# Two expert stages re-ordered around eight head groups of gated linear attention, with the keys' low halves ahead of the decayed scores

## The reference, cut to what matters

```python
x = x + 0.5 * ffn(layernorm(x)); x = x + attn(layernorm(x)); x = x + 0.5 * ffn(layernorm(x))

def ffn(h):                                     # 64 experts, 8 kept
    scores = softmax(h @ router_weight.T + router_bias)
    w, idx = top_k(scores, 8)
    return h * w.sum() + scatter(w, idx) @ expert_bias

def attn(h):                                    # 32 heads in 8 groups (one key and value head each), 16 chunks of 128
    q, k = rope(h @ Wq.T), rope(h @ Wk.T);  v = h @ Wv.T
    dt = softplus(h @ Win.T + dt_bias);  g = -dt * exp(A_log_bias);  G = cumsum(g in the chunk)
    xc = v * dt
    y = (q k.T * exp(G_i - G_j) masked) @ xc + (q * exp(G)) @ state
    state = state * exp(G_last) + (k * exp(G_last - G)).T @ xc
    return (rms_norm(y) * gnorm_w * silu(h @ Wg.T)) @ Wo.T
```

## Time and profile before

| | |
|---|---|
| median of 3 runs | 1793.26 us (1790.17 to 1793.82) |
| profiled execution | 1792.12 us, span 1790.3 us |
| TensorE busy | 1680.6 us (94%), mean granted clock 0.975 |
| VectorE, ScalarE, GpSimd busy | 1442.7, 1138.8, 1209.0 us |
| the chain that ended last | TensorE 68%, GpSimd 15%, issue 7%, VectorE 5%, ScalarE 5% |

### The profile page before, as it was taken

The page is one execution under the profiler, slowest core; times in us unless marked ns, Lnnn a source line. Parts: engine busy times, 40 slices in busy tenths (PEclk is TensorE's granted clock), DMA queues, the critical chain, the costliest instruction groups (busy, mean ns, idle before and its releaser), DMA issues.

```text
span 1790.3 us, 34879 instructions
## 1 busy us (share of the span) xinstructions
PE 1680.6 (94%) x11652; PEld 964.7 (54%) x11652; DVE 1442.7 (81%) x3157; ACT 1138.8 (64%) x3012; POOL 1209.0 (68%) x1139
## 2 busy tenths in 40 slices
PE   5667999999999999999999999999999999999976
PEld 4443555555555555555555555555555555555544
DVE  6984888888887878888897878787887888788876
ACT  5445666666666667666676666666766667666643
POOL 1225767776777768777777777776777768777633
PEclk9778999999999999999999999999999999999997
DMA  4110101110110101110121102110111111110002
GB/s 176 36 35 20 48 19 60 45 45 21 34 56 34 48 25 54 48 48 19 34 68 36 37 19 70 38 42 25 43 60 30 36 33 57 37 36 21 23 1 94
DMA packets 38481, 76.69 MB, mean 43 GB/s; under 512 B 4768, under 2 KB 5792, under 8 KB 37152
## 3 DMA queue, kind: packets, MB, share of 16 engines
q1 hardware_dynamic: 38304, 74.47, 13.2%
HBM read 69.99 MB, written 4.46 MB: 42 GB/s over the span
## 4 chain that ended last, share of the span: by engine, by line
PE 68%; POOL 15%; issue 7%; DVE 5%; ACT 5%; DMA 0%; SPq 0%; POOLq 0%; ACTq 0%; DVEq 0%
PE B L298 21%; PE B L300 21%; PE B L299 21%; PE B L784 3%; POOL WL L1099 3%; POOL QS L1105 2%; POOL PL L1140 2%; POOL ROWS L1118 1%; POOL WVF L1128 1%; POOL RR L1147 1%; POOL QL L1110 1%; ACT XN L417 1%; ACT QS L893 1%; ACT PF L931 1%; POOL WVL L1136 1%
## 5 line engine op out<-in xcount | busy, mean ns | idle before, releaser
L1140 POOL TENSOR_TENSOR PL<-PF,PH 128x512 bf16<-128x512 f32 x128 | 158.1, 1235 | 314.3 <-ACT PH L937 314.3
L298 PE MATMUL B<-WH,XTH 128*128 128x512 bf16 (+1 forms) x1024 | 282.6, 300 | 2.2 <-POOL WL L1099 2.2
L299 PE MATMUL B<-WL,XTH 128*128 128x512 bf16 (+1 forms) x1024 | 282.5, 300 | 0.0
L300 PE MATMUL B<-WH,XTL 128*128 128x512 bf16 (+1 forms) x1024 | 282.5, 300 | 0.0
L937 ACT ACTIVATE PH<-PF 128x512 bf16<-128x512 f32 x128 | 80.8, 631 | 276.0 <-DVE PF L1309 276.0
L298 PE MATMUL B<-XTH,WH 128*128 128x512 bf16 x640 | 243.3, 380 | 4.2 <-DVE QF L1275 3.5
L1105 POOL TENSOR_TENSOR QS<-QS,SIN 128x512 f32<-128x512 f32 x160 | 204.4, 1278 | 61.6 <-ACT QS L893 61.6
L299 PE MATMUL B<-XTL,WH 128*128 128x512 bf16 x640 | 243.3, 380 | 0.0
L300 PE MATMUL B<-XTH,WL 128*128 128x512 bf16 x640 | 243.1, 380 | 0.0
L1359 DVE SCALAR_TENSOR_TENSOR YF<-B,RR,G 128x128 f32<-128x128 f32 x512 | 144.0, 344 | 73.1 <-POOL RR L1147 73.1
L1309 DVE SCALAR_TENSOR_TENSOR PF<-B,DT,PF 128x128 f32<-128x128 f32 x512 | 143.4, 341 | 68.9 <-PE B L300 56.4
(11 more groups left out here) (158 smaller groups left out, 4464.8 us busy)
## 6 DMA issues: line engine op xcount, KB each, us to landing
ROWS<-rows_dram SPq DMA_DIRECT2D x128, 256.0 KB, 3.3
STAGE<-in_wall SPq DMA_DIRECT2D x112, 256.0 KB, 2.8
ACC<-in_x SPq DMA_DIRECT2D x4, 1024.0 KB, 9.4
out<-ACC SPq DMA_DIRECT2D x3, 1024.0 KB, 3.9
COS<-in_cos SPq DMA_DIRECT2D x1, 1024.0 KB, 13.7
SIN<-in_sin SPq DMA_DIRECT2D x1, 1024.0 KB, 16.4
out<-ACC SPq DMA_DIRECT2D x4, 256.0 KB, 2.0
EBF<-in_eb SPq DMA_DIRECT2D x1, 256.0 KB, 4.3
```

Of the source, the lines that this page charges most:

```text
L298: nc.tensor.matmul(out_, ah, bh, start=first, stop=False)
L299: nc.tensor.matmul(out_, ah, bl, start=False, stop=False)
L300: return nc.tensor.matmul(out_, al, bh, start=False, stop=last)
L1140: nc.gpsimd.tensor_tensor(PL[:, n % 2, :], PF[:, :], PH[:, n % 2, :], ALU.subtract).then_inc(pl_ready.sem, 1)
```

## The change

Steady steps: VectorE's `keys_lo` goes ahead of `decayed`. The three ring banks are renamed, the order of output banks in the last block changes. In the last group statistics of blocks NB and NB + 1 move into chunks 6 to 11, normalising, turns, copies and logits of block NB into chunks 12 to 15, and in these `wv_hi` goes behind `state_hi`. XN and XNT get buffers of their own (TXN, TXNT) in the memory of XTH and XTL.

```diff
@@ VectorE, ScalarE, TensorE: step
+                if s == 3 and now:
+                    keys_lo(g, b + 1)
                 if nxt:
                     decayed(g, n + 1)
...
-                if s == 3 and now:
-                    keys_lo(g, b + 1)
...
-                if last and n >= NCH - BLK:
-                    dve_stats(dve, 0, NB, (n - NCH + BLK,))
+                if last and BLK + 2 <= n < 2 * BLK + 2:
+                    dve_stats(dve, 0, NB, (n - BLK - 2,))
+                if last and 2 * BLK + 2 <= n < 3 * BLK:
+                    dve_stats(dve, 0, NB + 1, (2 * (n - 2 * BLK - 2), 2 * (n - 2 * BLK - 2) + 1))
...
+                if last and n == NCH - 4:
+                    act_normalise(act, 0, NB, (0, 1, 2))
+                if last and n == NCH - 3:
+                    act_turned(act, NB, (0,))
+                    act_normalise(act, 0, NB, (3,))
+                if last and n in (NCH - 3, NCH - 2):
+                    act_turned(act, NB, (n - NCH + 4,))
                 if nxt:
                     p_hi(g, n + 1)
...
-                if nxt:
+                ending = last and n >= NCH - BLK
+                if nxt and not ending:
                     wv_hi(g, n + 1)
...
                 square(g, n)
                 state_hi(g, n)
+                if nxt and ending:
+                    wv_hi(g, n + 1)
...
+                if last and n == NCH - 3:
+                    pe.wait_ge(out_free.sem, out_free.at(g, 2 * BLK + 1))
+                    pe_turn(pe, NB, (0,))
                 read_state(g, n)
+                if last and n in (NCH - 3, NCH - 2):
+                    pe_turn(pe, NB, (n - NCH + 4,))
+                if last and n == NCH - 1:
+                    pe_logits(pe, NB, (0,))
```

```diff
+            for i in range(BLK):
+                sp.dma_start(ACC[:, i, :], x[0][:, i, :]).then_inc(x0_landed[i].sem, 16)
+            sp.dma_start(IDF[:, :], masks[:, 2 * P:3 * P]).then_inc(id_landed.sem, 16)
...
+            nc.gpsimd.memset(WH[:, NPIECE - 1, :], 0.0).then_inc(zero_ready.sem, 1)
...
+            pe.wait_ge(zero_ready.sem, 1)
+            for i in range(28):
+                nc.tensor.matmul(B_T[:, :], WH[:, NPIECE - 1, 0:P], WH[:, NPIECE - 1, :], start=True, stop=True)
+            pe.wait_ge(id_landed.sem, 16)
+            pe_turn(pe, 0)
+            pe.wait_ge(router_landed.sem, 32)
+            pe_logits(pe, 0)
+            pe_turn(pe, 1)
+            pe.wait_ge(const_dve.sem, 6)
+            pe.wait_ge(const_act.sem, 2)
+            for k in range(NB):
+                if k:
+                    pe_turn2(pe, k - 1)
+                pe_weights(pe, k)
+                if 1 <= k < NB - 1:
+                    pe_turn(pe, k + 1)
+                pe_mix(pe, k)
+                if k + 1 < NB:
+                    pe_logits(pe, k + 1)
+                if k:
+                    pe_dt(pe, k - 1)
+                if k == NB - 1:
+                    pe.wait_ge(f_l.sem, f_l.at(NB - 1, 0))
+                    for item in range(2):
+                        fill(0, 0, item, None, True, 0)
...
+            pe_turn2(pe, NB - 1)
+            pe_dt(pe, NB - 1)
+            pe_sums(pe, 0)
+            for item in range(2, NFILL):
                 fill(0, 0, item, None, True, 0)
+                if item % 2 == 0:
+                    pe_rows(pe, item // 2 - 1)
+                elif item < NFILL - 1:
+                    pe_sums(pe, item // 2)
@@ ScalarE
             for k in range(NB):
                 act_exp(act, k)
+                if k:
+                    act_normalise(act, 1, k - 1)
+                    act_turned2(act, k - 1)
+                if k == 0:
+                    act_turned(act, 1)
+                act_weights(act, k)
+                if 1 <= k < NB - 1:
                     act_turned(act, k + 1)
+                for i in (2 * k, 2 * k + 1):
+                    split_hi(0, i)
                 if k + 2 < NB:
                     act_normalise(act, 0, k + 2)
@@ GpSimd
             for k in range(NB):
+                for i in range(BLK):
+                    pool_sum(pool, k, i)
+                pool_rstd(pool, 1, k)
+                pool.wait_ge(f_s8.sem, f_s8.at(min(k + 1, NB - 1), 0))
+                for i in (2 * k, 2 * k + 1):
                     split_lo(0, i)
@@ VectorE
+            dve_stats(dve, 0, 2)
+            dve_gate(dve, 0)
             dve.wait_ge(const_act.sem, 2)
...
+            dve_stats(dve, 0, 3)
+            dve_mixed(dve, 0)
+            dve_stats(dve, 1, 0)
+            for k in range(1, NB):
                 dve_gate(dve, k)
+                dve_turned2(dve, k - 1)
+                dve_mixed(dve, k)
+                if k == NB - 1:
+                    dve_dt_in(dve, 0)
                 dve_stats(dve, 1, k)
+            dve_dt(dve, 0)
+            dve_turned2(dve, NB - 1)
```

```diff
@@ TensorE
             for f in range(NB, 2 * NB):
                 if f + 1 < 2 * NB:
+                    if f == NB:
+                        pe.wait_ge(st_ready.sem, st_ready.at(KVH - 1, cs_event(NCH - 2)))
+                        pe.wait_ge(inter_read.sem, inter_read.at(KVH - 1, in_event(NCH - 1)))
                     pe_turn(pe, f + 1)
+                    pe_logits(pe, f + 1)
...
                 pe_weights(pe, f)
                 pe_mix(pe, f)
-                if f + 1 < 2 * NB:
-                    pe_logits(pe, f + 1)
+                if f == NB:
+                    project_out(KVH - 1, NCH - 1, True)
@@ ScalarE
+            act_normalise(act, 0, NB + 1)
             zt_hi(KVH - 1, NCH - 1)
             for f in range(NB, 2 * NB):
+                if f == NB:
+                    act_turned(act, f + 1)
                 act_exp(act, f)
+                if NB < f < 2 * NB - 1:
                     act_turned(act, f + 1)
                 act_weights(act, f)
+                if f + 2 < 2 * NB:
+                    act_normalise(act, 0, f + 2)
@@ VectorE
+            dve_stats(dve, 0, NB + 2, (0, 1))
+            dve_gate(dve, NB)
             zt_lo(KVH - 1, NCH - 1)
             add_out(KVH - 1, NCH - 2, True)
+            dve_stats(dve, 0, NB + 2, (2, 3))
+            dve_mixed(dve, NB)
+            dve_gate(dve, NB + 1)
             add_out(KVH - 1, NCH - 1, True)
+            dve_stats(dve, 0, NB + 3)
+            dve_mixed(dve, NB + 1)
+            dve_gate(dve, NB + 2)
+            dve_gate(dve, NB + 3)
+            dve_mixed(dve, NB + 2)
+            dve_mixed(dve, NB + 3, (0, 1))
+            dve_last(dve, NB + 3, (2, 3))
```

More of the change, by code:

```diff
@@ L132, in build @@
         ACC = sb("ACC", [P, NCH, HID])
+        with ExitStack() as over:
+            TXN = over.enter_context(nc.sbuf_tensor("TXN", [P, 3, BLK, HID], F32))
+            TXNT = over.enter_context(nc.sbuf_tensor("TXNT", [P, BLK, HID], F32))
         XTH = sb("XTH", [P, KT, L], BF16)
@@ L414, in act_normalise @@
                 act.wait_ge(f_acc.sem, f_acc.at(f - 2, 3))
             A = chunks_of(f)
[L416 to L422 removed]
+            for i in chunks:
+                into = xnt(f, i) if w else xn(f, i)
+                nc.scalar.activation(into, A[:, i, :], ACT.Identity, bias=NMR[:, w, f % 2, i:i + 1],
+                                     scale=RSTD[:, w, f % 2, i:i + 1]).then_inc(f_xn[w].sem, 1)
@@ L423, in pe_turn @@
+        def pe_turn(pe, f, chunks=range(BLK)):
+            for i in chunks:
                 pe.wait_ge(f_xn[0].sem, f_xn[0].at(f, i))
@@ L426, in pe_turn @@
                     pe.wait_ge(f_xtl.sem, f_xtl.at(f - 2, i))
+                elif f == 1:
+                    pe.wait_ge(f_xnt.sem, f_xnt.at(0, i))
+                elif f == NB and i:
+                    pe.wait_ge(f_xnt.sem, f_xnt.at(NB, i - 1))
                 elif f >= NB + 2:
                     pe.wait_ge(f_ax.sem, f_ax.at(f - 2, i))
-                elif f % NB:
-                    pe.wait_ge(f_xnt.sem, f_xnt.at(f - 1, i))
+                into = BANK[0] if f == NB else mix(f, i)
@@ L440, in pe_logits @@
-        def pe_logits(pe, f):
-            if f:
+                if f > NB:
+                    act.wait_ge(f_lg.sem, f_lg.at(f - 1, 0))
+                nc.scalar.activation(xnt(f, i), (BANK[0] if f == NB else mix(f, i))[:, :], ACT.Copy).then_inc(f_xnt.sem, 1)
+        def pe_logits(pe, f, chunks=range(BLK)):
+            if f == NB:
+                pe.wait_ge(f_xnt.sem, f_xnt.at(NB, BLK - 1))
+            elif f:
                 pe.wait_ge(f_l.sem, f_l.at(f - 1, 0))
-            for i in range(BLK):
+            for i in chunks:
@@ new lines, in rows, with pair, dve_dt_in, act_dt_exp @@
+            return ap.rearrange("p (c h) -> p c h", c=2 * BLK)
+        def pair(T, q):
+            return T[:, 2 * q * BH:2 * (q + 1) * BH]
+        def dve_dt_in(dve, q):
+            dve.wait_ge(d_dot.sem, d_dot.at(2 + q, 0))
+            nc.vector.tensor_tensor(rows(SPX), rows(pair(DOTS, q)), by_head(DTB), ALU.add).then_inc(d_x.sem, 1)
+            dve.wait_ge(d_x.sem, d_x.at(q, 0))
```

(25 more changed lines are left out.)

368 lines of the change are left out of this document (160 added, 208 removed).

## The result

The changed kernel takes 1752.24 us (median of 4 runs, 1750.69 to 1753.34), the kernel before, in runs beside it, 1793.47 (1790.17 to 1793.82): ratio 0.9773, 95% interval 0.9757 to 0.979, 41 us faster. Forecast were 1741 and a gain of 52. The time lies between the bounds given (1726 to 1764) but outside the forecast's own range of 1730 to 1748; 11 us of the gain did not come.

A forecast was written before the change was run, and what follows sets the result against it. TensorE was taken to bound only the stretch from 200 to 1691 us. Head 25, keys 9 and tail 18 sum to 52 off 1792.12, giving 1740.1, as a median 1741 us; own range 1730 to 1748 (0.60), bounds 1726 to 1764.

The forecast's parts named there:

- The keys: Steady steps: keys_lo before decayed removes eight TensorE waits of 1.21 us; 9.0 us taken, bounds 0 and 9.7.
- (b): Steady steps: the removed KDL waits are replaced by waits for weighted values or weights; 1750 us, chance 0.08.
- (c): Steady steps: keys_lo waits for ScalarE's KDH and delays the decayed scores in all 32 blocks; 1814 us, chance 0.03.
- The first stage's start: First expert stage: gate 0 waits for the third megabyte, starting at 19.4, 0.9 us sooner; zero multiplications taken as 0.
- The rounds: First expert stage: rounds of 15.9, 17.1, 17.1 and 15.7 us, ending at 85.2 instead of 106.4.
- rival (a): First expert stage: chunk hand-overs set rounds of 21 us, gaining 12 instead of 25; 1754 us, chance 0.13.
- From the last statistics to the keys: Head, after the rounds: series about 8.0 us each, keys turned 43.3 us after the statistics, at 128.5 instead of 153.84.
- The last four chunks: End of the long stretch: weighted values behind squares and statistics moved earlier give 2.0 us; bounds minus 1 and plus 3.
- The second expert stage: Tail: earlier first gate and re-ordered rounds end at 1771.5; 18 us gained, last four chunks' 2.0 included, bounds 9 and 22.
- rival (d): Expert stages don't start early: gate 0 waits for loads to 24, added turns and logits delay last chunks; 1751 us, chance 0.07.

The follow-up runs named there:

- the keys' edit alone: The kernel before with one edit, keys_lo ahead of decayed in the ordinary steps: 1778.07 us, ratio 0.9919.
- the run with all edits: Changed kernel plus GpSimd out of both series, second series later, 38 zeros in the second stage, seventh block's output in quarters, last quarters sent as done: 1744.84 us.

## Why the forecast was right in kind and 11 us off in size

**The keys.** Right in mechanism and too small: 13.1 instead of 9.0, above the bound of 9.7. The term counted the idle time before TensorE's products, eight times 1.21, and not the waits of its weight loads, 15 of them and 12.4 us. Rivals (b) and (c) did not occur: no other wait took the place, and KDH is early enough.

**The first stage's start.** Right in what holds gate 0. It was forecast for 19.4 behind the third megabyte; it came at 20.12 (18.84 to 20.36 in the runs of the same order) with the load as its releaser, and the zeros are worth nothing. The gain of 0.9 is not shown: in the old order, which waits for the logits instead, gate 0 came at 20.32 in one profile and at 18.58 in another (the keys' edit alone).

**The rounds.** Right. 16.50, 17.35, 17.30 and 16.2 us against 15.9, 17.1, 17.1 and 15.7, so rival (a), 21, is out. That the new fused product does not slow GpSimd's sums also held: four sums take 4.97 us beside it, 1.24 each as alone.

**From the last statistics to the keys.** Wrong, and the largest miss: KDL came 51.7 us behind the end of the statistics, where 43.3 to the turned keys, with the 1.4 from there to KDL, make 44.7. The step that failed is the price of the series, "about 8.0" each. The instructions are priced rightly (8.0 each with GpSimd held back), but the sum had them alone, while GpSimd's list, moved by the same change, put eight products beside them. By the forecast's own times the low halves end at +14.0 instead of +10.5, the second series at +27.0 instead of +21.1. Holding GpSimd back shows 4.5 us of the 7.0. The prediction had the row that warned (a product of 3.63 beside GpSimd) and applied it to the sums only. Of the 2.5 us that stay in that run, 0.6 stand at the second series' end (+21.7) and 1.9 behind it, where the moved GpSimd products hold four rotary steps of VectorE (1.37, 0.86, 1.55 and 0.98 us instead of 0.68).

**The last four chunks.** Wrong: the 2.0 us did not come, and undoing the edit of the weighted values costs 0.3. Which wait sets these chunks no run separates.

**The second expert stage.** Gate 4 starts 10.5 us sooner against the last turn, as forecast. The rounds behind it were to become 6.6 us shorter than the 55.8 of before and became 1.1 longer. The 7.7 us that are missing from there (56.9 instead of 49.2) grow in four places, by the forecast's own times: by the end of gate 5 it is 1.3 late (three steps beside GpSimd's sums last 0.73, 0.68 and 0.96 us instead of 0.17, 0.42 and 0.40); by the end of the second fused product 4.6, the half level in the logits, which the two runs whose level did not fall there don't show; by VectorE's end 6.2 (GpSimd's last sum 6.0), since the last two scaled products take 2.81 us where 1.4 was taken from rows without GpSimd beside them; and the end another 1.7, since the last sum was taken to be followed by 2.4 us as in the kernel before, where a quarter took 2.0 us to land, while now it takes 2.8, with a megabyte and three of the quarters sent close together:

```profile
out<-ACC SPq DMA_DIRECT2D x1, 1024.0 KB, 3.9
out<-ACC SPq DMA_DIRECT2D x4, 256.0 KB, 2.8
```

Sending the megabyte sooner took this from 4.1 to 3.8, and the run with all edits, which also sends the quarters as they are done, has 2.7.

**The chances.** The forecast's own range, at 0.60, was missed. The time lies at the price of rival (d), 1751, by chance: gate 0 did not wait until 24, and the turns put into the last chunks delayed nothing. It would have been 1756 had the keys not given 4.1 us more than forecast. What came, the forecast's mechanism with steps priced too low, had no line of its own.

## What to carry to other kernels

A step's duration from a row holds only beside the neighbours that it had there: when a change moves GpSimd's list, lay the new list against VectorE's before adding up, and price each VectorE step of a held form (here two inputs in SBUF, or a scaling from SBUF to SBUF) that meets a GpSimd product at that product's length. Moving the products elsewhere gives back only part, here 4.5 of 6.2 us. A wait removed from an in-order queue is often handed to its next member, so follow the queue two members on; of the three re-orderings tried here the later series paid 1.7 us of the 3 to 5 expected, the quarters 0.3, and gate 0 put first lengthened its round by 5 us. The idle time before a late operand is a lower bound: eight waits of 1.21 us were worth 13, so look at the weight loads' waits too. And where two runs of one program differ, look for the place where the clock fell before calling one of them better.

## What the runs showed of the hardware that was not expected

- A VectorE step on one SBUF input is held as well: the scaling L654 takes 0.28 us alone and 1.24 beside a GpSimd product, like the products with two inputs. RECIPROCAL (1.75 us at 104.24, with GpSimd's products from 104.44), MAX8 (0.61 at 1709.25, inside GpSimd's sums of 1708.09 to 1713.23) and products with an operand in PSUM (0.68) are not.
- With the same instructions of the second expert stage, TensorE's granted clock fell to the half level at the first block's mix in some runs and at the third block's logits in others (0.50 from 1715 to 1720 us in the changed kernel). Gates 5 to 6 took 12.5, 14.4 to 14.6 or 16.0 to 16.1 us by it, the largest difference between their spans inside this stage.
- At that first mix the level fell after TensorE had been idle for 0.57 and 0.69 us (with GpSimd out of the series) and stayed after the same 0.57 and 0.69 us in another run (with the second series later).
- The third block's last aggregate, behind the third megabyte, starts between 18.55 and 20.06 us in the nine runs of one order, which is more than most of the edits of this stage are worth.
